# A rational-softmax attention block: item banks emptied between a product and the older sum

## The reference, cut to what matters

```
xc    = x @ W[cat] + b[cat]
q,k,v = split(xc @ w_qkv.T)                       # 16 heads of 32
s     = q @ k.T / sqrt(32) - |i - j| * slope[h]   # causal: -1e4 above the diagonal
num   = 0.5 * (1 + s * rsqrt(1 + s*s))
attn  = num / (sum(num) + 1e-6) @ v
x     = x + attn @ w_out.T
r     = x + relu(x @ W1[lang] + b1) @ W2[lang] + b2
z     = layernorm(r) * gamma[lang] + beta[lang]
x     = x + (int8(z) @ int8 weights) * scales + bias
```

## Time and profile before

| | before |
|---|---|
| median of 3 runs | 2193.9 us (2190.4 to 2200.6) |
| profiled execution | 2191.5 us |
| its span, first to last instruction | 2189.8 us |
| mean granted TensorE clock | 0.929 |
| TensorE matmul busy | 1778.5 us, 81% |
| VectorE busy | 1736.8 us, 79% |
| ScalarE busy | 1709.5 us, 78% |
| GpSimd busy | 1693.0 us, 77% |

### The profile page before, as it was taken

How to read it: one execution, slowest core, us unless ns; L and a number is a source line. 1 busy time by engine, 2 the same in 40 slices (tenths; PEclk the granted TensorE clock), 3 DMA queues, 4 the chain that set the end, 5 groups by cost and what they waited for, 6 DMA issues and landing times.

```text
span 2189.8 us, 29394 instructions
## 1 busy us (share of the span) xinstructions
PE 1778.5 (81%) x10699; PEld 901.2 (41%) x10702; DVE 1736.8 (79%) x1730; ACT 1709.5 (78%) x1842; POOL 1693.0 (77%) x723
## 2 busy tenths in 40 slices
PE   5678888888887879997786887888888788988764
PEld 4455434333333445654343443433333344444231
DVE  4248888988999878977555777899999898879748
ACT  0037999999999978977554777999999998889652
POOL 3037899999989968877554776899998998889648
PEclk9899999999999989999988999999999999999889
DMA  5411111111111112212211212011111113112146
GB/s 182 150 50 41 46 31 31 42 38 35 36 35 45 31 56 64 60 41 61 68 44 47 81 50 64 24 44 40 36 32 36 41 31 90 42 57 58 59 160 204
DMA packets 122139, 130.38 MB, mean 60 GB/s; under 512 B 27372, under 2 KB 77548, under 8 KB 121580
## 3 DMA queue, kind: packets, MB, share of 16 engines
q1 hardware_dynamic: 121996, 128.51, 21.0%
HBM read 45.89 MB, written 22.54 MB: 31 GB/s over the span
## 4 chain that ended last, share of the span: by engine, by line
PE 34%; ACT 28%; DVE 17%; issue 11%; POOL 4%; SPq 3%; DMA 2%; DVEq 0%; POOLq 0%; ACTq 0%
ACT yb L765 11%; ACT gb L730 8%; ACT yb L767 8%; DVE gb L1094 6%; PE sc L943 6%; PE ov L921 6%; DVE gb L1159 5%; PE dn L921 5%; PE it L859 4%; PE it L866 4%; PE it L839 3%; SPq L479 3%; POOL oT L724 2%; PE it L843 2%; DMA area<-in_x_dram 1%
## 5 line engine op out<-in xcount | busy, mean ns | idle before, releaser
L691 POOL TENSOR_TENSOR yb<-yb 128x1024 f32<-128x1024 f32 x544 | 1503.6, 2776 | 384.8 <-DVE gb L1159 369.0
L1159 DVE TENSOR_TENSOR gb<-sc,yb 128x1024 f32<-128x1024 f32 x544 | 663.3, 1219 | 170.2 <-ACT yb L767 165.6
L765 ACT ACTIVATE yb<-sc 128x1024 f32<-128x1024 f32 x544 | 550.7, 1012 | 265.0 <-PE sc L943 157.9
L1094 DVE TENSOR_TENSOR gb<-gb,yb 128x1024 f32<-128x1024 f32 x544 | 753.8, 1386 | 0.0
L943 PE MATMUL sc<-qmv,kst 128*128 128x512 f32 (+3 forms) x1280 | 479.7, 458 | 175.0 <-DVE gb L1159 160.7
L767 ACT ACTIVATE yb<-yb 128x1024 f32<-128x1024 f32 x544 | 575.6, 1058 | 17.2
L730 ACT ACTIVATE gb<-gb 128x1024 f32<-128x1024 f32 x544 | 566.2, 1041 | 0.0
L943 PEld LDWEIGHTS sc<-qmv,kst 128*128 128x128 f32 x1280 | 230.6, 202 | 492.9 <-DVE gb L1159 342.8
L921 PE MATMUL ov<-gb,vv 128*32 128x512 f32 (+3 forms) x2560 | 320.0, 584 | 30.2 <-DVE den L1108 22.6
L921 PE MATMUL dn<-gb,ones 128*32 128x512 f32 (+3 forms) x2560 | 310.5, 568 | 0.0
L839 PE MATMUL it<-hT,wT 128*128 128x512 f32 x496 | 249.4, 608 | 14.4 <-ACT area L742 8.5
(11 more groups left out here) (118 smaller groups left out, 1087.9 us busy)
## 6 DMA issues: line engine op xcount, KB each, us to landing
qmv<-stage SPq DMA_DIRECT2D x384, 64.0 KB
kst<-stage SPq DMA_DIRECT2D x384, 64.0 KB
area<-in_x_dram SPq DMA_DIRECT2D x58, 256.0 KB, 2.8
out_dram<-oT SPq DMA_DIRECT2D x32, 256.0 KB, 3.2
wT<-wT_d SPq DMA_DIRECT2D x7, 768.0 KB, 4.3
x_d<-area SPq DMA_DIRECT2D x16, 256.0 KB, 2.6
z_d<-area SPq DMA_DIRECT2D x16, 256.0 KB, 2.9
gb<-z_d SPq DMA_DIRECT2D x4, 1024.0 KB, 12.2
```

Of the source, the lines that this page charges most:

```text
L691: pool.tensor_tensor(y, y, y, ALU.mult).then_inc(s_y2, 1)
L765: act.activation(yview(n), sc[:, n % SLOTS], ACT.Square).then_inc(s_s2, 1)
L1094: dve.tensor_tensor(gview(n), gview(n), yview(n), ALU.add).then_inc(s_num, 1)
L1159: dve.tensor_tensor(gview(n), sc[:, n % SLOTS], yview(n), ALU.mult).then_inc(s_g, 1)
```

## The change

On VectorE, the function `scored(k)` did everything for a pair at once: product, sum of the pair two before, maxima (L1047) and inversion (L1112). It ran behind the items of its pair and ahead of the output. Now it is two functions. `product(k)` has the product, and the output follows it directly. `rest(k)` has the sum, the maxima and the inversion, and runs ahead of the next pair's product, behind the items that came in between. On ScalarE the items are emptied between L767 and L730 instead of behind L730.

```diff
@@ ScalarE
                     act.activation(yview(n), yview(n), ACT.Abs_reciprocal_sqrt, bias=1.0).then_inc(s_y, 1)
-                    if n >= NUM_LAG:
-                        one_plus_g_squared(n - NUM_LAG)
                     for job in after_pair.get(k, []):
                         d = b if g is ending else b - 1
                         after(d, job, bases[0] + job.index, zs_before(d, job.name[1]))
+                    if n >= NUM_LAG:
+                        one_plus_g_squared(n - NUM_LAG)
@@ VectorE
-                def scored(k):
+                def product(k):
 
                     n = G * PAIRS + k
                     if n >= GRING:
                         dve.wait_ge(s_pv, products_until(n - GRING))
                     dve.wait_ge(s_y, n + 1)
                     dve.tensor_tensor(gview(n), sc[:, n % SLOTS], yview(n), ALU.mult).then_inc(s_g, 1)
+                    for u in emptied.pop(k, []):
+                        c = g.last_unit.index(u % UNITS)
+                        if u >= 0:
+                            output(G, hg, g, u, c, g is opening and c == 0)
+                        else:
+                            output_prev(G, prev_hg, u, c)
+
+                def rest(k):
+
+                    n = G * PAIRS + k - 1
                     if n >= NUM_LAG:
                         numerator(n - NUM_LAG)
                     while reduced and reduced[0][0] < k:
...
                     for c, prev in inverts.get(k, []):
                         invert(G - 1 if prev else G, c)
 
+                emptied = {}
                 k = None
                 for e in g.events:
-                    if e[0] in ("qk", "pv") and k is not None:
-                        scored(k)
-                        k = None
                     if e[0] == "qk":
+                        if k is not None:
+                            rest(k)
+                            product(k)
                         k = e[1]
...
                     elif e[0] == "pv":
                         u = e[1]
-                        if u < 0 and not carry:
-                            continue
-                        if u % UNITS in g.last_unit:
-                            c = g.last_unit.index(u % UNITS)
-                            if u >= 0:
-                                output(G, hg, g, u, c, g is opening and c == 0)
-                            else:
-                                output_prev(G, prev_hg, u, c)
-                if k is not None:
-                    scored(k)
+                        if (u >= 0 or carry) and u % UNITS in g.last_unit:
+                            emptied.setdefault(k, []).append(u)
+                rest(k)
+                product(k)
```

More of the change, by code:

```diff
@@ L1206, in _ @@
             for_groups(group)
-            for n in range(TOTAL - NUM_LAG, TOTAL):
+            for n in range(TOTAL - NUM_LAG - 1, TOTAL):
                 numerator(n)
```

## The result

The changed kernel takes 2272.8 us (median of 4, 2271.9 to 2276.9) against 2192.9 us: a ratio of 1.036, 95% interval 1.033 to 1.039. It is 80 us slower, where 35 were predicted; the range ended at 2258. The span of the profiled execution grew from 2189.8 to 2271.1 us.

What follows compares the result with a forecast made beforehand. ScalarE bounds the plain groups, TensorE the closing one, no engine the joining one. Plain +40, opening +5, closing -2, joining -12, ending +4 make +35 us on 2191.5, forecast 2227 us, range 2195 to 2258.

Steps and rivals of the forecast that it cites:

- the mechanism: VectorE's L1094 and GpSimd's L691 take turns, first come first done: about 1.1 us for the one, 1.9 for the other.
- the discount: Late sums' price reduced for slack: 6 of 15 us in plain groups, a third kept in opening, little showing in joining.
- ending: Ending group: 29 places, and 60 moved ScalarE instructions push L730 and so L1094 back: +4 us (-5 to +11).
- prologue and last phase: Outside the pair groups: order kept but for one L1094 moved by a slot, so nothing.
- The places in a plain group: Plain group: 18 places where L1094 comes late, 12 at 0.65 and 6 at 1.2 us: 15 us a group.
- I take 6 as given back: Plain group: earlier output releases TensorE sooner, and ScalarE's idle stretches swallow 6 us of the places' delay.
- A third of the 14: Opening group: 25 places, a third of the 14 us that the same sum gives: +5 us (-3 to +14).
- much slower: Whole kernel: nothing swallowed, joining gives nothing, +99 us at most; half way 2258; TensorE's clock may fall; chance 0.16.
- Closing: TensorE is the bound: Closing group: TensorE idle 20.2 us in all, the saving a part of that: -2 us (-8 to +4).
- Joining: Joining group: shorter TensorE waits for ScalarE's and VectorE's items, -25 us in all, half taken: -12 (-25 to +5).
- The reciprocal's "+1": Plain group: L1112 waiting for its DMA now blocks a product; with operand DMAs starting sooner, about +1 us.
- half way point of 2258: Whole kernel: half way from the forecast to the much slower case's maximum of +99 us, used as the range's upper end.

Runs made afterwards that it cites:

- output_only: Kernel before with only the output (L1107, L1108 and the two of the group before) moved ahead of the sum on VectorE: 2198.8 us, ratio 1.002.
- half squares: GpSimd's square L691 cut to half of each pair, other half left unsquared: 2178.0 us on the kernel before, 2174.4 us on the changed kernel.
- late_only: Kernel before with only the maxima and the inversion moved one product earlier on VectorE: 2210.9 us, ratio 1.008.
- half_no_late: Changed kernel with maxima and inversion put back one product later outside the joining group, and GpSimd's square on half of each pair: 2153.9 us.
- items_only: Kernel before with only the items emptied ahead of the sum on VectorE where no output stands between two products: 2281.2 us, ratio 1.039.
- half_after: Changed kernel with GpSimd's square L691 on half of each pair, the other half left unsquared: 2174.4 us, ratio 0.992.
- dve_only: Changed kernel with ScalarE's order put back (L730 ahead of the emptied banks), VectorE keeping its new order: 2286.3 us, ratio 1.042.
- no_late: Changed kernel with the maxima (L1047) and the inversion (L1112) put back one product later outside the joining group: 2264.0 us, ratio 1.033.

## Why the prediction was off

The sign and the mechanism were right, and so was that the plain groups carry most of the loss and the joining one alone gains. The sum was 46 us short, and the closing group's sign was wrong. The step that failed is the discount: a late sum was priced rightly at its place, and then much of the price was taken off for slack that the engines were thought to have. Term by term, as the groups came out:

| | predicted | measured |
|---|---|---|
| plain, four | +40 | +54.8 |
| opening | +5 | +18.7 |
| closing | -2 | +8.3 |
| joining | -12 | -7.2 |
| ending | +4 | +6.0 |
| prologue and last phase | 0 | +0.7 |
| sum | +35 | +81.3 |

The miss is 14.8 us in the plain groups, 13.7 in the opening, 10.3 in the closing, 4.8 in the joining and 2.0 in the ending one.

**The places in a plain group: right.** 0.6 us at a single place, 18 places, 15 us forecast. There are 18 short L691 in each plain group (none before) and ScalarE waits 14.7 to 15.5 us for L1094. The other signs of the mechanism came too: L691's mean fell below 2600 ns and L1094's rose above 1450. Plain groups of 219 us did not: they last 222 to 225.

**"I take 6 as given back": wrong, and the main error in the plain groups.** ScalarE's waits for TensorE shrank by only 2.9 us in the first plain group, and by 2.5, 3.6 and 1.4 in the others. TensorE's own wait for L1108 did shrink, from 4.4 to 0.9 us there, as forecast. But the lead does not last. At two outputs of that group ScalarE's square starts 2.4 and 2.3 us sooner against its neighbours than before, and one or two pairs later 1.2 and 1.4 us of it go again: at the first L1112 waits for its DMA with a product behind it, at the second TensorE comes late from an item (L839) at the lower clock. With the place's own 0.6 to 1.2 us an output nets about nothing (an estimate from these steps). output_only, which has no early inversion, agrees: its four plain groups gain 3 us in all. The busy time of +1.8 us had no term at all.

**"A third of the 14" in the opening: wrong.** I reasoned that TensorE has slack and hides most of it. ScalarE's waits there, before and after:

```profile
ACT yb L765 <- PE sc L943: 33.7, 10, 21.9
ACT yb L765 <- PE sc L946: 31.7, 8, 23.2
```

```profile
ACT yb L765 <- DVE gb L1094: 38.2, 20, 21.3
ACT yb L765 <- PE sc L946: 31.1, 8, 23.3
ACT yb L765 <- PE sc L943: 12.3, 10, 3.2
```

The one long wait of 21 us changed its name, from L943 to L1094. Without it L1094 costs 16.9 us and L943 still 12.3 (11.8 before): nothing is hidden, and with 2.5 us of busy time it is the whole +18.7. But not all of this is the turn of L1094 and L691: with half squares the opening group is still 10.7 us longer (250.0 against 239.3), and 6.4 with the inversion put back (245.7). What makes those is not shown. In addition TensorE's clock fell: 0.95 to 0.90 over the group, and TensorE is busy 218.0 us for the matmuls that took 204.2. In slices of 20 us from the group's middle on (columns as in the windows by group; the mean granted clock is the third number from the end), before:

```profile
237.60:257.60 20.00, 18.11 (x117) 9.08 (x120) 19.57 (x19) 18.18 (x20) 17.42 (x7) 1.00 0.24 58
257.60:277.60 20.00, 15.85 (x96) 6.66 (x88) 16.62 (x16) 19.78 (x21) 19.10 (x7) 1.00 0.23 65
277.60:297.60 20.00, 14.93 (x81) 6.23 (x82) 17.77 (x17) 17.84 (x19) 17.52 (x7) 0.74 0.18 42
297.60:317.60 20.00, 17.87 (x116) 8.31 (x114) 18.32 (x18) 19.62 (x22) 18.36 (x7) 1.00 0.17 42
```

and after:

```profile
238.80:258.80 20.00, 18.99 (x81) 7.64 (x74) 16.45 (x15) 17.14 (x18) 16.02 (x7) 0.91 0.17 41
258.80:278.80 20.00, 18.06 (x121) 9.28 (x124) 17.33 (x15) 16.40 (x18) 15.27 (x7) 0.83 0.28 81
278.80:298.80 20.00, 15.75 (x96) 6.02 (x86) 16.79 (x14) 18.10 (x19) 15.67 (x7) 0.83 0.17 42
298.80:318.80 20.00, 16.57 (x68) 5.74 (x68) 16.58 (x16) 16.83 (x18) 12.95 (x6) 0.83 0.03 5
```

Before, one of these four slices has time at the lower of the two levels, 1.2 GHz; after, all four have (a mean of 0.83 is a third of the slice at half speed). The prediction named this only as a rider of the "much slower" case. The longer group goes with the lower clock over most of the kernels: late_only 246.0 us at 0.95, half_no_late 245.7 at 0.94, items_only 254.9 at 0.93, after 261.4 at 0.90; half_after, 250.0 us at 0.92, is out of line. How much of the 18.7 us is the clock's own, and how much the waits that brought it down, stays open: no run held the clock with the waits in place.

**"Closing: TensorE is the bound", -2: wrong.** ScalarE waits 28.7 us for L1094 there and the waits for TensorE shrink from 43.1 to 23.3. A late sum makes the square, the product and so TensorE's next scores late: its waits for L1159 went from 1.7 to 9.1 us. A busy share of 92% did not protect the group.

**Joining: half right.** TensorE's waits in this group, after, against the earlier trace rows:

```profile
PE it L866 <- ACT area L748: 14.4, 4, 5.4
...
PE sc L943 <- DVE gb L1159: 9.2, 9, 2.8
...
PE it L839 <- ACT area L742: 5.6, 3, 1.9
PE it L866 <- DVE stage L1023: 4.8, 2, 3.6
...
PE it L875 <- ACT area L745: 3.1, 4, 1.7
...
PE it L873 <- ACT area L742: 2.4, 3, 1.1
```

L742 and L745 give 8.3 us, ScalarE's part, and dve_only, which lacks that part, is 10 us longer in this group. L748 and L1023 give nothing, and the products now make TensorE wait 5.6 us more, of which I had said that little would show.

**The reciprocal's "+1": too low.** late_only puts maxima and inversion at +18 us by themselves, and no_late at 9 within the change, against 1 a plain group, 4 in all, in the forecast.

So one step was wrong in three places: a cost on ScalarE, VectorE and TensorE's common loop was discounted for slack elsewhere (6 of 15 in the plain groups, two thirds in the opening, all of it in the closing group). At full price plain is +64 with the reciprocal, opening +14, closing positive, which was my "much slower" case. The plain groups came to +54.8, between the forecast and that price, the opening above it; and the half way point of 2258 was already too low for the end of the range. How much of the opening's share is the slack, and how much the clock and what the half squares left over, stays open.

## What to carry to other kernels

Before moving an instruction with two SBUF inputs on VectorE, see which GpSimd instruction the same event releases: who is first holds the other up for its whole length, so the shorter and more urgent one belongs directly behind the event. When every engine waits for the same ring of pairs, count a delay of one of them at full price until a row shows the slack that swallows it, and take a saving only as far as the next wait. A half-size version of the rival instruction is a cheap test of such a conflict, and shows what the reordering would be worth without it.

## What the runs showed of the hardware

The turns are of whole instructions: a late L1094 (1.2 us alone) ends 1.08 us behind the end of L691, and L691 (1.9 us alone) takes 2.8 us with an L1094 in its front. Of the 544 L691 in each trace of before and after none lies between 2.0 and 2.7 us. An instruction that stands in for the other's turn is recorded as busy, which is why a kernel that lost 80 us shows VectorE at 1858.0 us instead of 1736.8 with the same work. The Trainium skill, page "GPSIMD Engine Reference", section "Key points", has the sharing of GpSimd's SBUF interfaces with VectorE's two-input instructions; these runs agree and add the price. And a reordering alone moved TensorE's mean granted clock in one stretch, the opening group, from 0.95 to 0.90 (0.90 in dve_only too).
